# A Mamba block between two mixtures of experts: POOL's product with B in one instruction a unit, and new orders of the engines

## The reference, cut to what matters

```python
x = x + 0.5 * ffn(layernorm(x))
x = x + attn(layernorm(x))           # 4 layers, then Wout
x = x + 0.5 * ffn(layernorm(x))

# one Mamba layer, inner width 256, 16 states
xp, z = split(rmsnorm(x) @ Win)
xc = silu(causal_conv4(xp) + conv_b)
dt, Bm, Cm = split(xc @ Wx)
delta = softplus(dt @ Wdt + bdt)
h[t] = exp(delta[t] * A) * h[t-1] + (delta[t] * xc[t]) * Bm[t]
y[t] = sum_n h[t, n] * Cm[t, n] + xc[t] * Dp
x = x + (y * silu(z)) @ Wblk
```

## Time and profile before

| | us |
|---|---|
| median of three runs | 4784.53 |
| lowest and highest | 4780.35, 4791.12 |
| the profiled execution | 4794.56 |
| its span | 4792.8 |

### The profile page before, as it was taken

The page is one execution under the profiler, slowest core; times in us unless marked ns, Lnnn a source line. Parts: engine busy times, 40 slices in busy tenths (PEclk is TensorE's granted clock), DMA queues, the critical chain, the costliest instruction groups (busy, mean ns, idle before and its releaser), DMA issues.

```text
span 4792.8 us, 49172 instructions
## 1 busy us (share of the span) xinstructions
PE 4067.6 (85%) x11584; PEld 1302.6 (27%) x11584; DVE 4166.1 (87%) x5567; ACT 3334.8 (70%) x4979; POOL 4289.3 (89%) x2281
## 2 busy tenths in 40 slices
PE   6786767899898988899889988899898989578869
PEld 2221222222232323232222322222232223122223
DVE  2568888999999999999999999999999999888853
ACT  3566666777777777777777777777777777666734
POOL 0559999999999999999999999999999999999960
PEclk9897877999999999999999999999999999788879
DMA  2224443443344334433443344334433443344310
GB/s 60 56 64 98 107 93 82 95 109 88 84 103 108 86 83 104 109 88 86 101 109 86 80 106 109 84 83 108 108 80 83 108 107 81 85 106 103 75 40 5
DMA packets 136616, 425.06 MB, mean 89 GB/s; under 512 B 15885, under 2 KB 35278, under 8 KB 135951
## 3 DMA queue, kind: packets, MB, share of 16 engines
q1 hardware_dynamic: 136335, 421.92, 37.9%
HBM read 145.04 MB, written 8.39 MB: 32 GB/s over the span
## 4 chain that ended last, share of the span: by engine, by line
PE 30%; DVE 20%; issue 17%; POOL 16%; ACT 11%; SPq 3%; DMA 2%; DVEq 0%; ACTq 0%; POOLq 0%
POOL work L821 8%; DVE work L642 7%; DVE dA_ps L642 6%; POOL work L811 6%; PE d_ps L383 6%; PE y_ps L354 3%; PE b_ps L370 3%; SPq L312 3%; PE a_ps L376 2%; ACT L518 2%; PE a_ps L370 2%; ACT dA_ps L493 2%; DMA bc_sb<-bc_rows 2%; PE s_ps L444 2%; PE b_ps L376 2%
## 5 line engine op out<-in xcount | busy, mean ns | idle before, releaser
L821 POOL TENSOR_TENSOR work<-dd_sb,bc_sb 128x1024 f32<-128x1024 f32 x1024 | 2410.7, 2360 | 66.0 <-issue 30.3
L493 ACT ACTIVATE dA_ps<-dd_sb,a_sb 128x512 f32<-128x512 f32 x2048 | 1364.5, 684 | 803.9 <-DVE work L642 441.4
L642 DVE TENSOR_TENSOR_SCAN work<-dA_ps,work 128x512 f32<-128x512 f32 x1408 | 1657.6, 1207 | 48.4 <-POOL work L821 29.2
L811 POOL TENSOR_TENSOR work<-work,bc_sb 128x1024 f32<-128x1024 f32 x704 | 1661.9, 2361 | 36.0 <-DVE work L642 35.3
L642 DVE TENSOR_TENSOR_SCAN dA_ps<-dA_ps,work 128x512 f32<-128x512 f32 x640 | 780.4, 1219 | 33.6 <-POOL work L821 20.3
L383 PE MATMUL d_ps<-sg_sb,wd_sb 128*128 128x512 f32 (+1 forms) x1536 | 756.7, 626 | 43.6 <-DVE sg_sb L720 43.6
L354 PE MATMUL y_ps<-work,sel_sum 128*32 128x512 f32 x4096 | 620.7, 681 | 111.2 <-POOL work L811 81.3
L370 PE MATMUL b_ps<-xT_sb,wg_sb 128*128 128x512 f32 (+1 forms) x768 | 445.3, 663 | 81.6 <-ACT sg_sb L517 81.3
L370 PE MATMUL a_ps<-xT_sb,wg_sb 128*128 128x512 f32 (+1 forms) x768 | 443.3, 660 | 34.3 <-ACT sg_sb L517 32.0
L647 DVE TENSOR_TENSOR work<-dA_ps,bc_sb 128x512 f32<-128x512 f32 x640 | 441.3, 690 | 18.6
L376 PE MATMUL a_ps<-xs_sb,wu_sb 128*128 128x512 f32 (+1 forms) x768 | 415.4, 623 | 26.2 <-DVE sg_sb L720 21.8
(11 more groups left out here) (101 smaller groups left out, 4105.1 us busy)
## 6 DMA issues: line engine op xcount, KB each, us to landing
dd_sb<-dd_src SPq DMA_DIRECT2D x512, 512.0 KB, 8.6
bc_sb<-bc_rows SPq DMA_DIRECT2D x256, 512.0 KB, 7.8
xr_sb<-in_L_attn_x SPq DMA_DIRECT2D x16, 256.0 KB, 6.1
bc_rows<-dbc_sb SPq DMA_DIRECT2D x128, 32.0 KB, 1.6
out<-xr_sb SPq DMA_DIRECT2D x16, 256.0 KB, 6.1
wg_sb<-in_L_ffn_Wg SPq DMA_DIRECT2D x1, 1376.0 KB
wu_sb<-in_L_ffn_Wu SPq DMA_DIRECT2D x1, 1376.0 KB
wd_sb<-in_L_ffn_Wd SPq DMA_DIRECT2D x2, 512.0 KB
```

Of the source, the lines that this page charges most:

```text
L493: act.activation(dA_ps[:, g % NDA, :], dd_sb[:, b, c, 0, :], ACT.Exp, scale=a_sb[:, l, b, j, c:c + 1]).then_inc(dA_ready, 1)
L642: dve.tensor_tensor_scan(dA if on_dve(i) else tile, dA, tile, 0.0, ALU.mult, ALU.add).then_inc(scanned, 1)
L811: pool.tensor_tensor(work[:, g % RING], work[:, g % RING], bc_sb[:, j, 0, :].unsqueeze(1).broadcast_to([128, 2, T]), ALU.mult).then_inc(po ...
L821: pool.tensor_tensor(work[:, g % RING], dd_sb[:, b, 2 * (i % 2):2 * (i % 2) + 2, 1, :], bc_sb[:, j, 1, :].unsqueeze(1).broadcast_to([128, ...
```

## The change

POOL's product with B takes a whole unit, 128x2048 (here BB0 to BB7). `dbu_ready` counts units now, and those who wait for it (the scan, and SP before dd and bc) are changed to match. Products with C stay as they are. All offset tables are new.

```diff
@@ -28,20 +28,20 @@
 
 
 W, PERIOD = 128, 32
-CORE = {"exp": -11, "scan": -1, "dbu": -8, "dve_prod": 0, "pool_prod": 15, "sum": 28, "y0": 87, "y1": 14}
-PREP = {"sq": -18, "ms": 10, "rms": 9, "xn": 12, "xp0": 13, "conv0": 16, "xp1": 25, "conv1": 25, "silu_xc": 28, "z0": 30,
-        "zc0": 29, "z1": 47, "zc1": 45, "silu_z": 60, "wx": 43, "dbc": 36, "rows": 23, "dt0": 51, "sp0": 54, "delta0": 58,
-        "du0": 66, "dt1": 66, "sp1": 72, "delta1": 82, "du1": 115, "dd0": 44, "dd1": 49, "bc": 31}
-NEAR = {"sq": 21, "ms": 28, "rms": 29, "xn": 41, "xp0": 42, "conv0": 44, "xp1": 54, "conv1": 54, "silu_xc": 60, "z0": 64,
-        "zc0": 60, "z1": 65, "zc1": 65, "silu_z": 92, "wx": 72, "dbc": 76, "rows": 35, "dt0": 77, "sp0": 84, "delta0": 87,
-        "du0": 90, "dt1": 95, "sp1": 93, "delta1": 108, "du1": 119, "dd0": 53, "dd1": 86, "bc": 47}
-POST = {"wblk": 88, "h": 95, "attn": 100, "x2": 104}
-POST_NEAR = {"wblk": 20, "h": 21, "attn": 43, "x2": 53}
-FFN_AT = {"gb": 1, "xs": 3, "g0": 4, "g1": 7, "g2": 8, "burst": 6, "u0": 11, "u1": 11, "u2": 18, "hh0": 14, "hh1": 15,
-          "hh2": 22, "down": 29}
-START = {"load": -130, "bn": -61, "nb": -50, "xtok": -46, "xt": -45, "xT": -44, "lg": -37, "lg_sb": -38, "mx": -35,
-         "mi": -33, "gap": -26, "we": -29, "eq": -19, "den": -23, "inv": -23, "comb": -17, "ct": -14, "gates": -14}
-END = {"yt": 26, "xo": 33, "bn": 41, "nb": 56, "xtok": 45, "ht": 75, "h": 80, "store": 83, "acc": 14}
+CORE = {"exp": -10, "scan": -1, "dbu": -3, "dve_prod": 1, "pool_prod": 16, "sum": 23, "y0": 89, "y1": 13}
+PREP = {"sq": -27, "ms": 6, "rms": 8, "xn": 12, "xp0": 11, "conv0": 13, "xp1": 13, "conv1": 24, "silu_xc": 27, "z0": 27,
+        "zc0": 27, "z1": 37, "zc1": 45, "silu_z": 59, "wx": 34, "dbc": 34, "rows": 10, "dt0": 42, "sp0": 50, "delta0": 58,
+        "du0": 80, "dt1": 65, "sp1": 67, "delta1": 76, "du1": 87, "dd0": 38, "dd1": 89, "bc": 38}
+NEAR = {"sq": 19, "ms": 23, "rms": 31, "xn": 40, "xp0": 37, "conv0": 42, "xp1": 46, "conv1": 54, "silu_xc": 59, "z0": 60,
+        "zc0": 60, "z1": 65, "zc1": 68, "silu_z": 91, "wx": 71, "dbc": 81, "rows": 15, "dt0": 76, "sp0": 85, "delta0": 88,
+        "du0": 94, "dt1": 78, "sp1": 86, "delta1": 102, "du1": 117, "dd0": 32, "dd1": 85, "bc": 23}
+POST = {"wblk": 78, "h": 91, "attn": 98, "x2": 104}
+POST_NEAR = {"wblk": 16, "h": 22, "attn": 50, "x2": 49}
+FFN_AT = {"gb": -3, "xs": 4, "g0": -1, "g1": 2, "g2": 3, "burst": 5, "u0": 9, "u1": 11, "u2": 13, "hh0": 15, "hh1": 15,
+          "hh2": 22, "down": 23}
+START = {"load": -130, "bn": -60, "nb": -54, "xtok": -51, "xt": -48, "xT": -47, "lg": -42, "lg_sb": -41, "mx": -41,
+         "mi": -40, "gap": -34, "we": -29, "eq": -24, "den": -24, "inv": -25, "comb": -23, "ct": -18, "gates": -19}
+END = {"yt": 20, "xo": 26, "bn": 53, "nb": 63, "xtok": 61, "ht": 77, "h": 80, "store": 78, "acc": 12}
 
 
 def phase_table():
@@ -306,7 +306,7 @@
                         sp.wait_ge(du_ready, 2 * k + b + 1)
                         if k > 0:
                             sp.wait_ge(dA_ready, 32 * (k - 1) + 16 * (b + 1))
-                            sp.wait_ge(dbu_ready, HALVES * (k - 1) + 8 * (b + 1))
+                            sp.wait_ge(dbu_ready, UNITS * (k - 1) + NJ * (b + 1))
                         for c in range(NG):
                             rows = dd_src[SEL * c:SEL * (c + 1), b, :, :].rearrange("p a t -> p (a t)")
                             sp.dma_start(dd_sb[:, b, c, :, :].rearrange("p a t -> p (a t)"),
@@ -316,7 +316,7 @@
                         k, w = at
                         sp.wait_ge(bc_stored, 32 * (k + 1))
                         if k > 0:
-                            sp.wait_ge(dbu_ready, HALVES * (k - 1) + 2 * (NJ + j) + 2)
+                            sp.wait_ge(dbu_ready, UNITS * (k - 1) + NJ + j + 1)
                             sp.wait_ge(pool_prod, pool_products(k - 1, 2 * (NJ + j) + 1))
                             if dve_products(k - 1, 2 * (NJ + j) + 1) > 0:
                                 sp.wait_ge(dve_prod, 2 * dve_products(k - 1, 2 * (NJ + j) + 1))
@@ -638,7 +638,7 @@
                     g = 32 * k + i
                     dA, tile = dA_ps[:, g % NDA, :], work[:, (g // 2) % RING, g % 2, :]
                     dve.wait_ge(dA_ready, g + 1)
-                    dve.wait_ge(dbu_ready, g // 2 + 1)
+                    dve.wait_ge(dbu_ready, g // NG + 1)
                     dve.tensor_tensor_scan(dA if on_dve(i) else tile, dA, tile, 0.0, ALU.mult, ALU.add).then_inc(scanned, 1)
                 if (at := part_at(t, CORE["dve_prod"], 4)) and on_dve(at[2]):
                     k, w, i = at
@@ -810,16 +810,15 @@
                     pool.wait_ge(scanned, 2 * g + 2)
                     pool.tensor_tensor(work[:, g % RING], work[:, g % RING],
                                        bc_sb[:, j, 0, :].unsqueeze(1).broadcast_to([128, 2, T]), ALU.mult).then_inc(pool_prod, 1)
-                if at := part_at(t, CORE["dbu"], 8):
-                    k, w, i = at
-                    u, g = i // 2, HALVES * k + i
-                    b, j = u // NJ, u % NJ
+                if at := part_at(t, CORE["dbu"], 16):
+                    k, w, u = at
+                    b, j, g = u // NJ, u % NJ, HALVES * k + 2 * u
                     pool.wait_ge(dd_loaded[b], 64 * (k + 1))
                     pool.wait_ge(bc_loaded[j], 16 * (k + 1))
                     if g >= RING:
                         pool.wait_ge(summed, (g - RING) // 2 + 1)
-                    pool.tensor_tensor(work[:, g % RING], dd_sb[:, b, 2 * (i % 2):2 * (i % 2) + 2, 1, :],
-                                       bc_sb[:, j, 1, :].unsqueeze(1).broadcast_to([128, 2, T]), ALU.mult).then_inc(dbu_ready, 1)
+                    pool.tensor_tensor(work[:, g % RING:g % RING + 2].rearrange("p h c t -> p (h c) t"), dd_sb[:, b, :, 1, :],
+                                       bc_sb[:, j, 1, :].unsqueeze(1).broadcast_to([128, NG, T]), ALU.mult).then_inc(dbu_ready, 1)
 
             def prep_pool(t):
                 for b in range(NBLK):
```

## The result

The changed kernel takes 4796.0 us (median of 7 runs, 4789.26 to 4799.95) against 4780.35 for the kernel before (7 runs beside them): a ratio of 1.0029, 95% interval 1.0018 to 1.0041. It is slower by 0.3%, where I had forecast 1% faster. The profiled execution took 4789.26 us, its span is 4787.5.

The account below looks back on a forecast made before the run. POOL was taken as the bound; -68 - 26 + 5 + 29 + 12 = -48 us took the profiled 4794.6 us to 4746.6, and the median, 10.0 lower, to 4736 us; range 4686 to 4798.

Parts of the forecast that it names:

- So POOL sets the rate and DVE comes 3 points behind.: Middle stretch: POOL, 97.6% busy, is the bound; DVE follows at 94.5%, so POOL's gain counts only while DVE and PE follow.
- second rival: DVE and PE become the bound whatever POOL does: 4775 to 4794 us, say 4784; chance 0.12.
- chance of 0.19 for a slower kernel: Chance given to a kernel slower by more than 0.2%: 0.18 + 0.02, less 0.01 for milder router stalls.
- The instruction: POOL's product with B: one of 2048 columns takes 4.50 us against 4.63 for two halves, 512 times: -68 us.
- SP's queue: SP's transfer order: bc2 and bc3 ahead of dd1 removes POOL's "issue" waits, -26 us (between 0 and 30).
- +5: SP's queue: dd0, now ahead of bc0, just lands in time for BB0: +5 us, ends 0 and 64.
- That wait cost 2.2 us in the stretch: nothing.: POOL's wait for ring slots before products with B: same sum awaited as before, so no added cost.
- since DVE never stood at a B product I cost this at nothing: DVE's first scan of a unit waits for 4.50 us of POOL work, not 2.32; POOL gives the same room: nothing.
- The router: Router block on POOL and DVE: new waits at cast and comb, 0.9 us a block, 32 times: +29 us (0 to 141).
- slow rival: DVE's lead doesn't grow, so the router's cast waits 3.3 us every time: 4813 us, 4848 with comb's wait; chance 0.18.
- The convolution: PE and DVE around the second convolution's matmul, moved ahead of the gates' broadcast: 0.2 us for 60 phases, +12 us.

Follow-up runs that it names:

- e1: Kernel before, each POOL product with B 992 columns wide in place of 1024: 4783.5 us, ratio 0.9996 to the kernel before.
- e3: Changed kernel with its new orders, but two products of 1024 columns, each with its own signal, in place of the wide one: 4792.9 us, ratio 1.0021.
- e11: Kernel before with two more zero-weight PE matmuls a phase on average, behind the down product of experts 1 and 5: 4874.2 us, ratio 1.0191.
- e17: Changed kernel with PE's sums over the states 256 columns wide in place of 512: 4718.1 us, ratio 0.9855 to the kernel before.
- e19: Changed kernel with PE's matmul that spreads the gates run in bf16 on three-part split gates, whole result computed: 4737.1 us, ratio 0.9893.
- e4: Changed kernel with a ring of eight halves in place of six: 4789.3 us, ratio 1.0007 to the kernel before.
- e14: Kernel before with two zero-weight PE matmuls a phase placed in PE's wait for xn, ahead of the first projection: 4789.1 us, ratio 1.0003.
- e5: Kernel before with each DVE scan 496 columns long in place of 512: 4769.7 us, ratio 0.9959.
- e16: Kernel before with PE's sums over the states 256 columns wide in place of 512: 4806.6 us, ratio 1.0051.
- e18: Kernel before with PE's sums 256 columns wide and POOL's products with B 992 columns wide: 4823.8 us, ratio 1.0014.

## Why the prediction was wrong, step by step

The measured 4796 lies just inside the stated range of 4686 to 4798, at its slow end, and the direction was wrong.

- **"So POOL sets the rate and DVE comes 3 points behind."** This step failed, and with it the sum. I read it from busy shares and from small waits. e1 took 70 us from POOL and gained nothing; e3 gave 68 us back to it and lost nothing. Work added to PE, the third in the list, did count in full (e11), and in the changed kernel relief of PE brought 78 and 59 us (e17, e19). My second rival, PE and DVE as the bound, had the nearest mechanism, at 0.12, and its sign came: POOL's share in the middle fell to 95.9% and DVE's waits for PE stayed, 117 us against 112. Its price, 4784, was within 12 us of the 4796 measured, but it had no loss in it, and the loss of 0.2% comes with the new orders (e3). The chance of 0.19 for a slower kernel stood on the router and on the width, neither of which was the cause, so no credit is due for it.
- **The instruction** (4.50 us, -68 us): right. 4.49 measured; POOL's busy time fell 72.8 us over the span. The rows gave 0.14 us for the fixed part (1.23 less 1.09), not the 0.13 used, which makes 73 us.
- **SP's queue** (-26 us, +5): the -26 came on the profile, and the +5 did not, since the 25.8 us of "issue" before products with B are 0.2 now and neither BB0 nor BB4 waits for a transfer. It was worth nothing for the time: POOL was not the bound.
- **"That wait cost 2.2 us in the stretch: nothing."** (the ring): wrong as a statement on POOL, 64.8 us. e4 shows that it was where POOL's spare time collected and hardly a cost: with the ring longer, the waits moved to DVE and the middle went no faster. **"since DVE never stood at a B product I cost this at nothing"**: DVE stood there for 23.9 us; e3, with the earlier signal for the first half, shows that this too was not worth time.
- **The router** (0.9 us a block, 0 to 4.4): right in size. The waits for max, max-index and the reciprocal are 17.4 us for 22 blocks, 0.8 us each; the one for the comparison, 4.8 us before, is gone. I had said that DVE's lead would grow; it fits, but I did not measure the lead. The comparison is no longer held either: 44 of them take 5.8 us in the changed kernel, 20.3 before, as its place behind the reciprocal suggested. The bound for the slow rival, 2.4 us a block, was never near.
- **The convolution** (0.2 us a phase): PE's wait for the first convolution went from 27.1 to 57.1 us, 0.7 us a phase. I had priced it as one of the slack. Two more waits of PE grew as much and were in no term of mine: for the block's output product before the first sum into `y_ps`, which stands five ticks earlier (3.7 to 36.0 us, and 36.1 in e3), and for the gating product (19.5 to 47.7). Which of the three, if any, makes the 0.2% that the new orders cost with halves (e3) was not tried.

Open: what holds the kernel before at 4783. POOL's time and PE's clock (a little, 0.97 to 0.98) could each be relieved without gain (e1, e14), and DVE's time gave a little (e5). For PE the question is not settled: e16 and e18 took work from it and gained nothing, but in e16 its busy time fell by only half of what was taken out, at the lower clock. That PE's order and its clock together hold this kernel stands as a rival that no run here rules out. A chain through ms, rms, xn and xp0, in which PE sits idle 2.1 us a phase on average (92.3 us in the stretch, 3.4 at most), would fit, but no run shortened it.

## What to carry to other kernels

A busy share of 97% need not name the bound: an engine in a coupled pipeline can be almost full and still have spare time, and the next few microseconds it saves turn up as waits of its own. Before a change, test the claim with the cheapest run there is, the same kernel with that engine's instruction a few per cent narrower; e1 would have told that this one had nothing to gain from POOL. An order set for one limit is not good or bad by itself: the new orders lost 0.2% on their own, saved the wide product from 1.1% down to 0.3%, and paid once PE was lighter.

## What the runs showed of the hardware

- **Less work on PE can be slower.** With the sums 448 wide in place of 512 the granted clock fell from 0.97 to 0.95 in the middle and the time rose by 0.45%; with 256 it was 0.94, and the time was not below the kernel before. In the trace of the kernel before one fall to half follows a wait of 3.37 us in which PE did nothing. The same 256 columns in the changed kernel left the clock at 0.97 and gave 1.6%.
- **A two-input POOL product costs 1.09 us for every 512 fp32 columns and 0.14 us fixed**, and this held out to 2048 columns (1.23, 2.32 and 4.49 us from start to start for 512, 1024 and 2048).
- **A matmul of 512 columns in bf16 took 0.22 us from start to start** (0.38 as recorded, one record), against 1.05 us in fp32 (two records of 0.65 to 0.69). Splitting a small fp32 operand in three bf16 parts, stacked in K, cost POOL four instructions of 0.21 to 0.25 us in every second phase, and the changed kernel got 59 us faster by it.
- **A DVE comparison of 128x32 with both inputs in SBUF** took 499 ns on average and up to 1253 in the kernel before, the longest beside a product on POOL, and 173 ns (189 at most) in the changed kernel, where it stands right behind the reciprocal for which POOL itself waits.
